# Values and keys laid out with the sequences taking turns: four partition-strided copies per axis in place of eight

## What is computed

```python
x = x + axial_linear_attention(group_norm(x), w_qkv0, w_out0, w_qkv1, w_out1)
x = x + criss_cross_attention(group_norm(x), Wq, bq, Wk, bk, Wv, bv, Wo, bo, sigma)
```

```python
q, k, v = split(x_seq @ w_qkv)            # per sequence and head
out = (q @ k.T * 256 ** -0.5) @ v         # no softmax
y = out @ w_out                           # both axes are summed
```

## Time and profile before

| | |
|---|---|
| median of 3 runs | 270.9 us (270.67 to 272.12) |
| the profiled execution | 270.76 us |
| its span, first to last instruction | 268.7 us |
| mean granted clock of PE | 0.946 |
| PE / PEld busy | 84% / 74% |
| DVE / ACT / POOL busy | 64% / 49% / 29% |
| DMA packets | 15,966, 13.97 MB |

### The profile page before, as it was taken

How to read it: one execution, slowest core, us unless ns; L and a number is a source line. 1 busy time by engine, 2 the same in 40 slices (tenths; PEclk the granted TensorE clock), 3 DMA queues, 4 the chain that set the end, 5 groups by cost and what they waited for, 6 DMA issues and landing times.

```text
span 268.7 us, 8193 instructions
## 1 busy us (share of the span) xinstructions
PE 226.2 (84%) x3276; PEld 198.3 (74%) x3276; DVE 172.9 (64%) x497; ACT 131.0 (49%) x321; POOL 78.2 (29%) x103
## 2 busy tenths in 40 slices
PE   0668767969999899999999999999999998666614
PEld 0547655958897789898989898889898887555613
DVE  7689764147765866587568747874778465743441
ACT  2452153426664566366546565656556555521230
POOL 8170006020442244225421642063315330034000
PEclk9999996899999999999999999999999999985865
DMA  6902110023003210340033003300310131001001
GB/s 247 327 32 49 33 41 2 0 74 86 5 0 89 71 39 0 84 109 3 5 86 105 0 10 86 99 0 15 87 54 0 21 86 51 2 0 41 0 0 39
DMA packets 15966, 13.97 MB, mean 52 GB/s; under 512 B 3536, under 2 KB 15440, under 8 KB 15952
## 3 DMA queue, kind: packets, MB, share of 16 engines
q1 hardware_dynamic: 15136, 12.47, 17.5%
q10 hardware_dynamic: 816, 1.31, 1.3%
HBM read 7.47 MB, written 2.10 MB: 36 GB/s over the span
## 4 chain that ended last, share of the span: by engine, by line
PE 51%; issue 14%; DVE 12%; SPq 8%; POOL 7%; ACT 5%; DMA 1%; POOLq 0%; DVEq 0%
PE bank L777 39%; SPq L243 7%; POOL rstd L298 3%; PE bank L857 2%; PE bank L835 2%; PE bank L866 2%; DMA v_wide<-k_v 1%; PE bank L911 1%; DVE y_out L599 1%; DVE ident L507 1%; PE bank L784 1%; POOL x1b L317 1%; POOL xt_lo L289 1%; PE bank L794 1%; ACT xn L351 1%
## 5 line engine op out<-in xcount | busy, mean ns | idle before, releaser
L298 POOL TENSOR_TENSOR rstd<-var_eps,minus_half 128x2 f32<-128x2 f32 x16 | 11.2, 700 | 105.9 <-DVE var_eps L535 105.9
L359 ACT ACTIVATE k_v<-bank 128x512 f32<-128x512 f32 x32 | 19.1, 598 | 37.0 <-PE bank L777 36.4
L351 ACT ACTIVATE xn<-bank,nbias,rstd 128x256 f32<-128x256 f32 x32 | 16.3, 561 | 26.8 <-DVE nbias L540 26.8
L370 ACT ACTIVATE kv<-bank,head_scale 128x256 f32<-128x256 f32 x64 | 25.1, 480 | 7.8 <-PE bank L835 7.8
L289 POOL TENSOR_TENSOR xt_lo<-xn,xn_hi 128x256 fp32r<-128x256 f32 x16 | 21.7, 1382 | 16.9 <-DVE xn_hi L544 16.9
L835 PE MATMUL bank<-v_wide,k_v 64*32 64x128 f32 x1024 | 18.4, 273 | 5.3 <-issue 3.9
L552 DVE TENSOR_TENSOR kv<-bank,block_mask 128x512 f32<-128x512 f32 x32 | 20.6, 685 | 3.4 <-PE bank L835 3.2
L857 PE MATMUL bank<-kv,q 64*32 64x128 f32 x1024 | 18.9, 275 | 2.5 <-ACT kv L370 1.1
L571 DVE TENSOR_TENSOR o_lo<-bank,o_hi 128x256 fp32r<-128x256 f32 x32 | 14.9, 510 | 9.3 <-ACT o_hi L385 9.3
L835 PEld LDWEIGHTS bank<-v_wide,k_v 64*32 64x32 f32 x1024 | 14.4, 105 | 7.1 <-issue 6.9
L777 PE MATMUL bank<-wout_hi,o_hi 128*128 128x256 f32 x64 | 18.7, 292 | 0.9 <-DVE o_lo L571 0.9
(11 more groups left out here) (163 smaller groups left out, 708.2 us busy)
## 6 DMA issues: line engine op xcount, KB each, us to landing
v_wide<-k_v SPq DMA_DIRECT2D x128, 32.0 KB, 2.0
x_in<-in_x_dram SPq DMA_DIRECT2D x8, 256.0 KB, 2.8
x_res<-in_x_dram SPq DMA_DIRECT2D x8, 256.0 KB, 2.8
out_dram<-y_out SPq DMA_DIRECT2D x8, 256.0 KB, 2.2
wqkv_in<-in_L_conv_w_qkv_dram ACTq DMA_DIRECT2D x1, 768.0 KB, 5.1
wqkv_in<-in_L_conv_w_qkv_dram SPq DMA_DIRECT2D x1, 768.0 KB, 7.2
wout_in<-in_L_conv_w_out_dram SPq DMA_DIRECT2D x2, 256.0 KB, 8.9
wl<-in_L_conv_Wo_dram ACTq DMA_DIRECT2D x1, 256.0 KB, 7.4
```

The costliest lines, as they stand in the source:

```text
L298: pool.tensor_tensor(rstd[k][:, :], var_eps[k][:, :], minus_half[:, :], ALU.pow).then_inc(rstd_ready[k], 1)
L351: last = act.activation(xn[k][:, c, :], norm_bank[k][:, c * TOKENS:(c + 1) * TOKENS], ACT.Identity, bias=nbias[k][:, c:c + 1], scale=rstd[ ...
L359: act.activation(k_v[:, axis, t, :, :].rearrange("p i d -> p (i d)"), src[:, :], ACT.Copy).then_inc(kv_taken, 1)
L370: last = act.activation(kv[axis][:, 1, :, :, :, head // 2, own].rearrange("p t c s e -> p (t c s) e"), kv_bank[1][:, :].rearrange("p (a e) ...
```

## The change

The tokens of a tile are arranged in turn: sequence 0 token 0, sequence 1 token 0, sequence 2 token 0, sequence 3 token 0, sequence 0 token 1, and so on, for each group of NEAR = 4 sequences. A sequence's tokens then stand on every fourth partition of k_v, in all groups of a tile alike, so one DMA fills one slot n of v_wide for 32 partitions (`n::NEAR`), with one row of 2 KB per partition: k_v and v_wide have their tile index moved inward, so that the two tiles' rows adjoin. `place_v` issues 4 DMAs per axis in place of 8.

The order is brought about where xn is split. DVE's `split_xn` reads xn[0] in the new order (`in_turn`: the innermost four elements are 16 elements apart, then 16 neighbours, then the next group) and writes contiguously; for k = 1 nothing changes. POOL's `turn` now waits for xn itself, does a 128 x 2 addition into pool_gate, copies xn to xt_hi in the new column order (runs of four neighbours), waits for its own copy, and then subtracts to xt_lo. `take_q` writes the queries back to the old order (its reads are contiguous, its writes go in steps of 64 bytes). Everything from `queries` on is as before.

```diff
@@ tiles and semaphores
+        pool_gate = sb("pool_gate", [P, CC])
-        k_v = sb("k_v", [P, 2, TT, 2, DIM])
-        v_wide = sb("v_wide", [P, 2, TT, NEAR, DIM])
+        k_v = sb("k_v", [P, 2, 2, TT, DIM])
+        v_wide = sb("v_wide", [P, 2, NEAR, TT, DIM])
-        res_loaded, turned = sem("res_loaded"), sem("turned")
+        res_loaded, turned, xt_hi_done = sem("res_loaded"), sem("turned"), sem("xt_hi_done")
+        def in_turn(ap):
+
+            return ap.rearrange("p (g n i) -> p g i n", n=NEAR, i=SIDE)
+
+        def dealt(ap):
+
+            return ap.rearrange("p (g i n) -> p g i n", n=NEAR, i=SIDE)
@@ SP, place_v
-                for s in range(SEQS):
-                    tokens = slice(s * SIDE, (s + 1) * SIDE)
-                    sp.dma_start(v_wide[tokens, axis, :, s % NEAR, :], k_v[tokens, axis, :, 1, :]).then_inc(v_placed[axis], 16)
+                for n in range(NEAR):
+                    sp.dma_start(v_wide[n::NEAR, axis, n, :, :], k_v[n::NEAR, axis, 1, :, :]).then_inc(v_placed[axis], 16)
@@ POOL, turn
-                pool.wait_ge(xn_hi_done[0], b + 1)
+                pool.wait_ge(xn_ready[0], b + 1)
+                pool.tensor_tensor(pool_gate[:, :], minus_half[:, :], minus_half[:, :], ALU.add)
                 for c in range(CC):
-                    pool.tensor_tensor(xt_lo[:, c, :].rearrange("p (w h) -> p w h", w=SIDE), by_axis(xn[0][:, c, :], 0),
-                                       by_axis(xn_hi[0][:, c, :].bitcast(FP32), 0), ALU.subtract)
+                    last = pool.tensor_copy(dealt(xt_hi[:, c, :]), xn[0][:, c, :].rearrange("p (h g n) -> p g h n", g=NEAR, n=NEAR))
+                last.then_inc(xt_hi_done, 1)
+                pool.wait_ge(xt_hi_done, b + 1)
                 for c in range(CC):
-                    last = pool.tensor_copy(xt_hi[:, c, :].rearrange("p (w h) -> p w h", w=SIDE), by_axis(xn_hi[0][:, c, :], 0))
+                    last = pool.tensor_tensor(dealt(xt_lo[:, c, :]), xn[0][:, c, :].rearrange("p (h g n) -> p g h n", g=NEAR, n=NEAR),
+                                              dealt(xt_hi[:, c, :]).bitcast(FP32), ALU.subtract)
                 last.then_inc(turned, 1)
@@ ACT, take_kv and take_q
-                act.activation(k_v[:, axis, t, :, :].rearrange("p i d -> p (i d)"), src[:, :], ACT.Copy).then_inc(kv_taken, 1)
+                act.activation(k_v[:, axis, :, t, :], src[:, :].rearrange("p (i d) -> p i d", i=2), ACT.Copy).then_inc(kv_taken, 1)
-                act.activation(q[:, 1 - i, :, :].rearrange("p c n -> p (c n)"), q_bank[i][:, :], ACT.Copy).then_inc(q_taken, 1)
+                act.activation(in_turn(q[:, 1 - i, :, :].rearrange("p c n -> p (c n)")), dealt(q_bank[i][:, :]), ACT.Copy).then_inc(q_taken, 1)
@@ DVE, split_xn
-                dve.tensor_copy(xn_hi[k][:, :, :], xn[k][:, :, :]).then_inc(xn_hi_done[k], 1)
+                xs, hi, lo = [tile[k][:, :, :].rearrange("p c n -> p (c n)") for tile in (xn, xn_hi, xn_lo)]
+                if k == 0:
+                    xs, hi, lo = in_turn(xs), dealt(hi), dealt(lo)
+                dve.tensor_copy(hi, xs).then_inc(xn_hi_done[k], 1)
                 dve.wait_ge(xn_hi_done[k], b + 1)
-                dve.tensor_tensor(xn_lo[k][:, :, :], xn[k][:, :, :], xn_hi[k][:, :, :].bitcast(FP32), ALU.subtract).then_inc(xn_split[k], 1)
+                dve.tensor_tensor(lo, xs, hi.bitcast(FP32), ALU.subtract).then_inc(xn_split[k], 1)
@@ PE, key_value
-                pe.wait_ge(v_placed[axis], 16 * SEQS * (b + 1))
+                pe.wait_ge(v_placed[axis], 16 * NEAR * (b + 1))
-                                                 k_v[rows, axis, t, 0, channels], v_wide[rows, axis, t, :, channels], start=True, stop=True)
+                                                 k_v[rows, axis, 0, t, channels], v_wide[rows, axis, :, t, channels], start=True, stop=True)
```

## The result

The changed kernel takes 275.3 us (median of 4 executions, 274.0 to 276.4), against 270.8 us for the kernel before in the same comparison. The ratio is 1.0158 (95% interval 1.0095 to 1.0221), that is +4.3 us (+2.6 to +6.0). The forecast was 277.3, range 271.2 to 279.0. The change makes the kernel slower, as forecast, by about two thirds of the amount.

A forecast was written before the change was run, and what follows sets the result against it. The prediction took PE, with DVE's split of the next batch's input beside it, to bound the kernel. 270.76 - 1.8 (copies) + 6.8 (DVE) + 1.1 + 0.4 (ACT) + 0 (POOL) = 277.3 us, range 271.2 to 279.0.

The forecast's parts named there:

- What bounds the kernel: Even loop: PE nearly gapless, DVE's split beside it on the path with 0.05 us slack; DMA waits at 59.70 and 93.42.
- DVE's read, +6.8 us: DVE's split for k = 0: strided read adds 1.02 us, 0.97 landing on PE in each of seven batches, +6.8 us.
- The failed term: DVE's copy in the split for k = 0: loses its fast pace, then pays the stride, 0.43 to 1.07 us, +0.64.
- The subtraction's term: DVE's subtraction in the split for k = 0: strided read raises it from 0.69 to 1.07 us, +0.38.
- Rival (c): POOL's turn beside DVE's split slows DVE by 0.19 us in seven batches, total 278.6; chance 0.13 shared with slow copies.
- ACT's write, +1.1 us in the loop: ACT's take_q: strided write adds 0.40 us, of which 0.18 is lost in each of six batches, +1.1 us.
- The start's +0.4: Start of the kernel: PE waits straight for the first q, so ACT's slower write costs +0.4 us.
- The copies, -1.8 us: SP's halved copies remove all DMA waits: 0.3 at 59.70, 1.0 at 93.42, 0.5 over six batches; bounds 0 and -3.0.
- POOL's turn, 0 at the start: POOL's turn at the start: shorter, but PE also needs wqkv_lo, delayed to 20.15; counted 0, bounds -1.0 and +1.0.
- The sum: Whole kernel: copies, DVE's read, ACT's write, the start and POOL's turn added to 270.76 us give 277.3 us.

## Why the prediction was right, point by point

- **What bounds the kernel.** Right. PE and DVE's split were side by side on the path with no more than 0.05 us between them: of the 0.69 us that DVE's two instructions grew, 0.66 stand on PE's timeline in front of 154.51. One wait outside the even loop was overlooked, the 1.20 us of the last batch.
- **DVE's read, +6.8 us.** Right in its mechanism, too large. Per batch 0.97 was forecast, 0.66 measured, 4.6 us in seven batches; the 0.66 holds 0.12 to 0.15 of POOL's copy beside it (next point), and the read by itself costs 0.49 to 0.56. The failed term is the copy: "I assume that the pace is lost with the stride, then the stride is paid: 0.69 + 0.38 = 1.07". It measured 0.64, so the fast pace was not lost; the stride slowed it by about the same factor as the subtraction. The subtraction's term held: 1.07 forecast, 1.04 to 1.07 measured without POOL's copy beside it.
- **Rival (c), POOL beside the split.** It held as well, on the other instruction than I had named: 0.12 to 0.15 us a batch, on the subtraction, from POOL's copy. With it the subtraction measured 1.17. "POOL's subtraction already ran beside L546 at 0.69" was true and no argument, since the change puts a copy there, and one that has begun when DVE's subtraction begins.
- **ACT's write, +1.1 us in the loop.** 0.18 a batch forecast, 0.25 to 0.27 measured: 1.6 us. The surcharge of q was 0.45 to 0.48, not 0.40. The start's +0.4 is +0.43 in PE's wait for the first q.
- **The copies, -1.8 us.** Measured -1.35 (-2.6 to -0.1), but not where it was counted: nothing in the even loop instead of 0.5, nothing at 59.70 instead of 0.3, 0.69 instead of 1.0 in batch 1, and 0.81 in the last batch, which the sum did not have. That the total is near is luck. In the changed kernel a wait of 0.15 us for y_out stands behind key_value, and none for the copies.
- **POOL's turn, 0 at the start.** It gave about 1 us, my lower bound: PE's 1.56 us of waiting for xt_hi is gone, and its first key_value starts at 33.01 against 33.53, with 0.43 more for q already in it (PE was at full clock from 14.5 us up to there in both). The reason for counting 0 failed: DVE was to end wqkv_lo at 20.15, but beside POOL's new turn its two instructions ahead of that end took 0.84 and 1.75 us instead of 1.60 and 2.15, and it ended at 18.64.
- **The sum.** 4.6 + 1.6 + 0.4 - 1.35 - 1.0 = +4.3 us, which is the measured ratio. The pieces come from different kernels, so the equality is partly luck. The second table gives nearly the same from one pair of traces: -0.52 at the start, +1.44 in two batches, +0.24 in batch 1, +3.64 in the four even ones and -0.81 in the last, +3.99 us. What is shown besides is that DVE's read alone (+4.1 us on the kernel before) is about the size of the whole loss.

## What to carry to other kernels

A layout that makes DMAs fewer has to be produced somewhere. Ask first whether the DMAs are waited for in the even part of the loop, and then which engine produces the order: here it was put on DVE and ACT, which were on the path, while POOL had 4 us to spare. Of a reordering, do the part that lies on an idle engine and leave the rest; half of this change, on axis 0 alone, was faster than both kernels. When work is moved on an engine that is off the path, look at what now runs beside it and which of the two starts first. Waits outside the even batches count too: what the four copies gained lay in batch 1 and in the last.

## What was not expected of the hardware

- DVE, float32, 512 elements per partition: a step of 8 bytes in the read is free; steps of 16 and 64 bytes cost the same, 0.69 to 1.04 and 1.07 us for two inputs, 0.43 to 0.64 for a copy. The strided copy is still faster than a contiguous two-input instruction. The 8-byte rows ran with POOL idle, the 16-byte ones beside POOL's subtraction; that subtraction added nothing to a contiguous read (0.69) or to one at 64 bytes (1.04 with it, 1.02 to 1.06 without).
- POOL's copy, begun 0.04 us earlier, slowed a two-input DVE instruction from 0.69 to 0.90 us; POOL's two-input subtraction at the same place, begun 0.11 us later, left it at 0.69 and was slowed itself (1.85 us for two, 1.41 behind DVE's split in the change). This does not show that a copy does more harm. At the end of the kernel before, a two-input addition of POOL was running when DVE's began, and DVE took 1.09:

```profile
245.54 1.09 DVE L546 TENSOR_TENSOR xn_lo<-xn,xn_hi 128x512 fp32r<-128x512 f32 x1
...
245.17 2.04 POOL L317 TENSOR_TENSOR x1b<-x,bias_out 128x256 f32<-128x256 f32 x2 [1.38 <-DVE y_out L599]
```

  In all three the instruction that begins later is slowed. No run here separates the order from the kind of instruction.
- An addition of 128 x 2 elements on POOL took 0.19, 0.37 or 0.59 us by what DVE did at the time.
- PE's granted clock drops for some microseconds early on in each of the 13 traces, between 28 and 35 us, between 40 and 52 us, or at both places. PE busy, PEld, DVE, ACT, POOL, then the mean clock, in two windows, first of the kernel before, then of the one with four copies:

```profile
34.00:42.00 8.00, 5.21 (x248) 4.16 (x231) 5.05 (x17) 4.01 (x11) 0.69 (x1) 0.99 0.12 35
42.00:50.00 8.00, 7.17 (x43) 5.90 (x31) 2.57 (x6) 3.56 (x9) 3.71 (x4) 0.59 0.01 2
```

```profile
34.00:42.00 8.00, 4.67 (x200) 3.72 (x200) 5.41 (x17) 3.97 (x10) 0.00 (x0) 1.00 0.10 35
42.00:50.00 8.00, 6.20 (x100) 5.53 (x101) 2.93 (x9) 4.23 (x10) 4.50 (x5) 1.00 0.01 2
```

In the first, after a stretch in which PE was busy for 5.2 of 8 us, the mean clock of 42 to 50 us is 0.59 of full speed, so most of it ran at the lower of its two levels (1.2 and 2.4 GHz); in the second it is 1.00 after 4.7 of 8 us, while its clock had been 0.88 between 20 and 34 us. In the chain of the kernel before, the 18 products from 44.24 take 5.04 us, and the same 18 in a later batch (125.81) take 2.84: about 2 us of device time hang on it, which is the size of the differences between executions of one kernel.
